# Second routing batch of three tiles instead of four, last tile's statistics first, and transposes that write the bank in the copy's order

## What is computed

```python
x = x + _L0_conv_ref(_ln_c(x), w3, w7, w15, w_mix)   # norm over 512 channels, three causal depthwise convs, mix to 32
t = _to_tokens(x)                                     # 2048 tokens of 512
t = t + _L0_ffn_ref(_ln_t(t), gate_w, w1, w2, w3)     # norm over the token, 8 experts, top 2 of them
x = _from_tokens(t, x)

def _L0_ffn_ref(hidden_states, gate_w, w1, w2, w3):
    router_logits = x @ gate_w.T
    routing_probs = softmax(router_logits)
    topk_w, topk_idx = top_k(routing_probs, 2);  topk_w = topk_w / sum(topk_w)
    h = silu(x @ w1[e]) * (x @ w3[e])
    out = sum over the two experts of topk_w * (h @ w2[e])
```

## Time and profile before

| | |
|---|---|
| Three runs | 861.5, 862.25, 862.29 us (median 862.25) |
| The profiled execution | 862.26 us, span in the trace 860.6 us |
| First stage (convolution steps) up to its last product | 0 to 159.0 us |
| From there to the first product of the expert stage | 159.0 to 202.2 us |
| Expert stage | 202.2 us to the end |
| Busy PE / DVE / ACT over the span | 809.1 / 354.5 / 326.8 us |

### The profile page before, as it was taken

The page is one execution under the profiler, slowest core; times in us unless marked ns, Lnnn a source line. Parts: engine busy times, 40 slices in busy tenths (PEclk is TensorE's granted clock), DMA queues, the critical chain, the costliest instruction groups (busy, mean ns, idle before and its releaser), DMA issues.

```text
span 860.6 us, 12441 instructions
## 1 busy us (share of the span) xinstructions
PE 809.1 (94%) x3852; PEld 670.5 (78%) x3853; DVE 354.5 (41%) x756; ACT 326.8 (38%) x489; POOL 221.1 (26%) x222
## 2 busy tenths in 40 slices
PE   4999999747999999999999999999999999999994
PEld 3887887646888888888888888888888888888883
DVE  5886657768122531244113512621172152135111
ACT  5873665541121622253125313521262171253211
POOL 4445210001111431133114221411251142142211
PEclk9999999756999999999999999999999999999998
DMA  8001232251811461146213711821273156111121
GB/s 311 14 26 49 83 90 62 76 205 28 314 25 37 147 206 25 24 129 224 37 24 80 273 27 34 303 51 24 34 260 83 37 160 193 24 24 37 26 35 24
DMA packets 35074, 83.19 MB, mean 97 GB/s; under 512 B 3056, under 2 KB 19696, under 8 KB 28912
## 3 DMA queue, kind: packets, MB, share of 16 engines
q1 hardware_dynamic: 26256, 63.18, 20.6%
q0 software_dynamic: 8224, 19.40, 12.1%
q10 hardware_dynamic: 576, 0.39, 0.2%
HBM read 64.88 MB, written 18.09 MB: 96 GB/s over the span
## 4 chain that ended last, share of the span: by engine, by line
PE 90%; DVE 5%; issue 2%; ACT 1%; DMA 1%; POOL 0%; ACTq 0%; DVEq 0%; POOLq 0%
PE bank L653 23%; PE bank L655 23%; PE bank L654 23%; PE bank L669 4%; PE bank L566 4%; PE bank L567 3%; PE bank L568 3%; PE bank L647 2%; PE bank L585 1%; PE bank L631 1%; PE bank L578 1%; DVE wc_lo L760 1%; PE bank L595 0%; DMA mixT<-in_mix 0%; ACT xs L426 0%
## 5 line engine op out<-in xcount | busy, mean ns | idle before, releaser
L653 PE MATMUL bank<-w_hi,xT_hi 128*128 128x512 f32 x576 | 229.6, 399 | 1.5 <-DVE xT_lo L932 1.5
L655 PE MATMUL bank<-w_hi,xT_lo 128*128 128x512 f32 x576 | 226.4, 393 | 0.0
L654 PE MATMUL bank<-w_lo,xT_hi 128*128 128x512 f32 x576 | 225.9, 392 | 0.0
L969 DVE TENSOR_TENSOR h<-bank,h 128x512 f32<-128x512 f32 x72 | 49.8, 691 | 301.6 <-PE bank L655 300.0
L653 PEld LDWEIGHTS bank<-w_hi,xT_hi 128*128 128x128 f32 x576 | 109.1, 189 | 23.6 <-DVE xT_lo L932 1.9
L655 PEld LDWEIGHTS bank<-w_hi,xT_lo 128*128 128x128 f32 x576 | 109.0, 189 | 23.7
L654 PEld LDWEIGHTS bank<-w_lo,xT_hi 128*128 128x128 f32 x576 | 109.2, 190 | 22.0
L497 ACT ACTIVATE h<-bank 128x512 f32<-128x512 f32 x72 | 43.0, 598 | 208.8 <-PE bank L655 208.4
L653 PE MATMUL bank<-w_hi,hT_hi 128*128 128x512 f32 x288 | 118.6, 412 | 0.0
L655 PE MATMUL bank<-w_hi,hT_lo 128*128 128x512 f32 x288 | 112.7, 391 | 0.0
L654 PE MATMUL bank<-w_lo,hT_hi 128*128 128x512 f32 x288 | 112.5, 391 | 0.0
(11 more groups left out here) (138 smaller groups left out, 919.4 us busy)
## 6 DMA issues: line engine op xcount, KB each, us to landing
w_raw<-in_units SPq DMA_DIRECT2D x48, 1024.0 KB, 4.9
out_x<-XT SPq DMA_DIRECT2D x17, 256.0 KB, 2.3
XT<-in_x SPq DMA_DIRECT2D x16, 256.0 KB, 6.6
xn_rows<-xnb SPq DMA_DIRECT2D x16, 256.0 KB, 2.3
xg<-xn_rows,gather_at POOLq DMA_INDIRECT x37, 3.4
out_x<-y,add_at POOLq DMA_INDIRECT x36
taps<-in_taps ACTq DMA_DIRECT2D x2, 160.0 KB, 4.5
mixT<-in_mix ACTq DMA_DIRECT2D x1, 48.0 KB, 4.0
```

Of the source, the lines that this page charges most:

```text
L653: pe.matmul(B[bank][:], stat_hi, hi, start=start, stop=False)
L654: pe.matmul(B[bank][:], stat_hi, lo, start=False, stop=False)
L655: return pe.matmul(B[bank][:], stat_lo, hi, start=False, stop=stop)
L969: dve.tensor_tensor(h[:, j, :], B[2 * j + 1][:], h[:, j, :], ALU.mult).then_inc(h_out, 1)
```

## The change

It has five parts.

1. The second batch is three tiles (8 to 10) and the third five (11 to 15). Mask, count, rank and hot rows of the second batch move one step ahead: mask in step 24, count, rank and hot rows in step 25.
2. On DVE, low_half 0 moves from step 24 to behind the last tile's `t_scales`; on ACT, high_half 1 moves from step 25 to behind the last copy `xnT`.
3. From step 26 on DVE's `t_stats` stands ahead of `t_join`, and PE's `t_moments` ahead of `logit`. Tile 15's moments go to bank 6 instead of 4, as tile 14's are still unread.
4. The hot rows of the last batch are built between the two halves of `hot` and `hot_token`.
5. `turn` writes the bank in the order (q, b, d) through a strided view, so `token_turned` reads and writes straight rows of 512.

```diff
-BATCHES = ((0, 8), (8, 12), (12, NT))
+BATCHES = ((0, 8), (8, 11), (11, NT))
...
 def moment_bank(n):
+    if n == NT - 1:
+        return 6
     return 7 if n < BATCHES[0][1] and n % 2 else 4
...
-                act.activation(xnT[n % 2][:].rearrange("p q (b d) -> p b d q", d=D),
-                               B[2 + n % 2][:].rearrange("p (b d q) -> p b d q", d=D, q=NQ),
-                               ACT.Copy).then_inc(xnT_out, 1)
+                act.activation(xnT[n % 2][:].rearrange("p q i -> p (q i)"), B[2 + n % 2][:], ACT.Copy).then_inc(xnT_out, 1)
...
-                for k, freed in ((0, 22), (1, 24)):
-                    if t == freed + 1:
-                        act.wait_ge(step_ps, freed)
-                        high_half(act, 0, k)
-
-            for k in range(2, UNITS):
+                if t == 23:
+                    act.wait_ge(step_ps, 22)
+                    high_half(act, 0, 0)
+
+            for k in range(1, UNITS):
                 high_half(act, 0, k)
...
+                turned = B[2 + n % 2][:].rearrange("p (q b d) -> p b d q", q=NQ, b=NB)
                 for b in range(NB):
-                    ins = pe.transpose(B[2 + n % 2][:, P * b:P * b + P], xnb[n % XB][:, b, :], ident[:])
+                    ins = pe.transpose(turned[:, b, :, :], xnb[n % XB][:, b, :], ident[:])
...
+                if t >= STEPS:
+                    for n in posts(t - 1):
+                        t_moments(n)
                 for n in posts(t - 3):
                     logit(n)
-                for n in posts(t - 1):
-                    t_moments(n)
+                if t < STEPS:
+                    for n in posts(t - 1):
+                        t_moments(n)
...
+                if t >= STEPS:
+                    for n in posts(t):
+                        t_stats(n)
                 for n in posts(t - 1):
                     t_join(n)
-                for n in posts(t):
-                    t_stats(n)
+                if t < STEPS:
+                    for n in posts(t):
+                        t_stats(n)
...
-                if t == 24:
-                    low_half(dve, 0, 0)
-
+
+            low_half(dve, 0, 0)
             mask_batch(len(BATCHES) - 1)
             rank_batch(len(BATCHES) - 1)
-            hot_rows(len(BATCHES) - 1)
...
             for k in range(2):
+                if k == 1:
+                    hot_rows(len(BATCHES) - 1)
```

More of the change, by code:

```diff
@@ L829, in hot_rows @@
                 pairs, n = slice(2 * first, 2 * stop), 2 * (stop - first)
-                for p in range(first // 2, stop // 2):
+                for p in range(first // 2, -(-stop // 2)):
                     dve.wait_ge(acc_st[p % 4], 16 * (p // 4 + 1))
```

## The result

Twenty runs of the changed kernel have a median of 865.43 us (862.16 to 867.2), beside 862.24 us (861.25 to 864.89) for twenty of the kernel before: 1.0027 of its time, 95% interval 1.0015 to 1.0039. It is slower by 0.3%; 863.5 us was forecast, with 860.3 to 867.5 as the range and 862.4 to 864.6 as the forecast's own part of it. The profiled execution of the kernel after took 867.17 us, span 865.5.

What follows compares the result with a forecast made beforehand. PE bounds the kernel, busy 94% of the span, with one clock hole at about 150 to 215 us. Terms -0.9, +4.6, -0.3, -0.9, -0.45 and -0.75 sum to +1.3: 863.5 us, range 860.3 to 867.5, own range 862.4 to 864.6.

Steps and rivals of the forecast that it cites:

- the sum: All terms from the upstream copies to the last batch added up: +1.3 us, giving 863.5 us.
- rival C: Second count and whole last convolution step run at the low clock: 865.4 us, or 866; chance 12%.
- DVE's two upstream waits, shorter by: DVE's waits for ACT's square root at 135.21 and 143.69 each shrink by 0.45 us through the shorter copy.
- PE idle ahead of the second count: In step 25 PE waits some 2 us for DVE's masks of the second batch, until 155.6.
- last convolution step: Step 25 on PE begins at 1.2 GHz and takes 7.1 us instead of 4.71, ending at 163.6.
- from 143.69 on DVE's unbroken series runs 0.9 us earlier: DVE's work up to the second batch's mask starts 0.9 us sooner, as two upstream waits shrink.
- the hole: Slices 8 to 10 of the profile before, about 150 to 215 us, where PE's granted clock is not full.
- The upstream gain: Shorter xnT copies ahead of DVE's series from 143.69: -0.9 us.
- Gets the full clock back after 4.8 us: PE in the last convolution step returns from 1.2 GHz after 4.8 us, as in the expert stage.
- Rival A: Clock holds through PE's wait in step 25: 861.6 us, or 859 if also in the last turns; chance 22%.
- Rival B: Transposes' strided write into the bank slows PE, up to 0.45 us per turn: 868 us taken, 870 at most; chance 14%.
- Rival D: Straight copy xnT is no cheaper, as the cost lay in reading the bank: 865.7 us; chance 5%.

Runs made afterwards that it cites:

- count behind: Kernel after with the second batch's count, rank and hot rows one step later, behind the last convolution step: 857.26 us, ratio 0.9955; run again, 859.01 us, ratio 0.9956.
- e4: Kernel after with 22 unread 128x256 products on PE ahead of the second batch's count: 862.0 us, ratio 1.0004.
- e5: Kernel after with unread 128x256 products on PE, 22 ahead of the second count and 9 ahead of the first: 861.03 us, ratio 0.9985.
- part 5 alone: Kernel before with only the strided write of the transposes and the straight copy: 861.54 us, ratio 0.9988.
- e6: Kernel after with second count, rank and hot rows one step later, plus 9 unread products ahead of the first count: 858.34 us, ratio 0.9944.
- e10: Kernel before with parts 1 and 2 of the change alone (batches and moved low halves): 867.22 us, ratio 1.0056.

## Why the prediction was right, and where it was lucky

The kernel is slower, and by the mechanism named: PE waits for the masks and then runs at the low clock. The size was right in part by luck. The median, 865.43, lies outside the forecast's own 862.4 to 864.6 and only inside the wider range; the change of 3.2 us by medians, 2.3 by the ratio, is more than the +1.3 of the sum. It happens to fall on the 865.4 of rival C, whose mechanism is not what ran. The predicted 863.5 lies in the lower level (middle 863.06; the upper one has 866.5), because the prediction knew nothing of levels. Step by step, with times of the profiled execution:

| Step of the prediction | predicted | measured |
|---|---|---|
| copy xnT | 0.60 | 0.60 |
| DVE's two upstream waits, shorter by | 0.45 each | 0.37; and 0.36 (2.10 to 1.74, count behind) |
| PE idle ahead of the second count | some 2 | 3.15 |
| mask of three tiles | 2.45 | 2.47 (156.57 to 159.04) |
| logits of step 24 on PE start | 150.4 | 154.54 |
| from there to the last convolution step | 6.1 | 6.37 |
| last convolution step | 7.1 | 6.11 (160.91 to 167.02) |
| its start to ACT's copy of tile 12 | 4.0 | 3.52 |
| rank of three, hot rows of three | 2.2, 0.87 | 2.24, 0.87 |
| ACT's copy to the last add | 4.4 | 4.21 |
| last add to norm of tile 14 | 2.95 | 3.20 |
| norm of tile 14 to norm of tile 15 | 4.0 | 4.07 |
| norm of tile 15 to the masks' first row | 5.40 | 5.42 (175.91 to 181.33) |
| from there to the token list | 12.03 | 12.03 (to 193.36) |
| token list to the first expert product | 14.23 | 14.21 (to 207.57) |

Every link behind step 24 is within 0.3 but two, and both of these are the clock that came back sooner than I took it to. The 6.37 hides two errors that cancel: DVE came to the mask sooner after the logits than I took it to, so the count starts 4.64 after them and not 5.2, and the count takes 1.73 at the low clock (159.18 to 160.91) where I put 0.9 at full clock. The link that failed stands ahead of them: "from 143.69 on DVE's unbroken series runs 0.9 us earlier". In this execution PE's step 24 ended 4.1 later than that. Some 0.9 of it was there early: the logits of step 22 stand at 130.86 instead of 129.97. That is a difference between executions and not the change: the other profiles of changed kernels have 129.38 to 130.65 there. The other 3.2 is the clock's fall at the first count, which the prediction never asked about: it looked for light stretches of PE where the change moved things and, from one profile's row of the clock, took PE as kept full by the convolution up to the hole. Of these 3.2 us, 2.4 arrive at the first expert product (e4 beside e5). Without the 2.4 and the 0.9 the profiled 867.17 would be 863.9, which lies in the lower level, 862.16 to 864.0. On the same count the change itself, wait and low clock with all that was saved, costs 2.0 us up to the first expert product (76.71 - 2.4 - 72.26), where the sum had 1.3.

**The upstream gain.** -0.9 was -0.73 where it could be seen (0.37 and 0.36), and real: part 5 alone had runs as low as 858.46.

**The last convolution step.** "Gets the full clock back after 4.8 us" was taken from one row of the expert stage. Here the first product at full clock (164.15) stands 3.2 us behind the step's first, hence 6.1 us and not 7.1. Elsewhere it was another time again: about 3 us in step 25 of e6, 4.2 in e10, 5 in step 23 of this profile, and 3.2 to 6.1 behind the first expert product. One row was no measure of it, and what sets it is not shown.

**Rival A**, the clock that holds, was priced at 861.6 and the last add at 163.0. The fillers produced that case in part: 861.4 to 862.0 at the lower level of the one kernel, 861.03 in the one without an upper level, with its last add at 162.72. Its other half, a clock that stays up in the last turns, is in no profile without fillers in the tail.

**Rival B** fell: turns in the convolution took 0.60 with the strided write (134.28) as without, and 0.36 from start to start in both kernels. The Trainium skill (PSUM — Partial Sum Buffer, Specifications) says that a pattern that is not contiguous slows matmuls significantly; for these transposes, 512 bytes from element to element, the trace does not agree. Where row and rule differ, the row holds. **Rival C** came true by half: the count did run at 1.2 GHz (1.05, and 0.83 us more than forecast), but the convolution step got its clock back after six products. **Rival D** fell with the copy's 0.60.

**What stays open.** Why the clock falls at the first count, in step 25 or behind the gate list in some executions and not in others. Which of these places makes the upper level of the kernel *before* is not known: no profile lies in that level, and no run with fillers was made of it. No kernel of the study was profiled in two levels.

## What to carry to other kernels

A wait that is put ahead of full-speed PE work can cost twice: its length with what it holds up, and the first microseconds behind it at half clock. Here, by the profiles, that was 4.1 and 2.1 us, for a change meant to shorten the path at its other end, and the cure was to put the small waiting products one step behind the large ones. Where single runs of a kernel fall in levels, look for every light stretch of PE ahead of large products, fill it with products that cost no time, and compare levels, and distances inside profiles, and not only medians. A price taken from one row of one profile, as the return of the clock was here, needs a range from several.

## What the runs showed of the hardware that I had not expected

- The same stretch can go either way. In step 25 of the kernel with the count behind, PE had the logits, 0.77 of waiting, a small product and 0.74 of waiting; in one execution the next product took 0.47 (clock 1.00 throughout), in another 0.77 (clock 0.77 in the microsecond from 153, 0.50 in the next). Six unread products there, 0.95 us, made six runs of six lie within 1.0 us.
- Thirty-two products of 128x84 in a row, PE busy all the while, stood ahead of a fall to 0.50 in five profiles (0.63 for a product of 128x512) and ahead of full clock (0.39) in seven, at the same place of the program.
- In the tail with filler products PE counted as busy for 5.62 of 6 us (transposes, logits and products of 128x128), and the granted clock was 0.50 all the while; within 14 of the same small products in one row, 3.27 us, it came back to 1.00.
- Four transposes of 128x128 into a bank with 512 bytes from element to element took 0.60, as with straight rows, while ACT's copy of 128x512 with that step in its write took 1.05 and straight 0.60: the same reordering was free on PE and cost 0.45 on ACT.
